# First attention stage: ScalarE's instructions put in another order within a group of steps

## The chip, the cores and the metric

One NeuronCore of a Trainium2 chip runs the whole program. The metric is the device time of one execution in microseconds (us); the figure for a kernel is the median over several executions.

## The reference, cut to what matters

The input is 16 sequences of 256 tokens with 128 features, in float32.

```python
x = L0_attn_hidden_states                    # (16, 256, 128)
x = _layernorm(x + _L0_attn_ref(x, ...))     # first attention
x = _layernorm(x + _L0_ffn_ref(x, ...))      # two layers of local attention and a gated MLP
```

The first attention works on a gated convolution of its input and takes a softmax over each chunk of 64 keys by itself:

```python
h = _dynamic_conv(x)                         # three taps, times a gate made from the mean over tokens
q, k, v = heads(h @ w_q.T), heads(h @ w_k.T), heads(h @ w_v.T)   # 16 query heads, 4 key/value heads, 64 wide
scores = jnp.einsum('bhqd,bhckd->bhcqk', q, kc) * scale
w = jax.nn.softmax(scores, axis=-1)          # over the 64 keys of one chunk
chunk_out = jnp.einsum('bhcqk,bhckd->bhcqd', w, vc)
out = (chunk_out * sum_w).sum(axis=2) / (sum_w.sum(axis=2) + 1e-09)
return out @ w_o.T
```

## The kernel before, in words

The program has two stages. `stage_a` (L342) is the first attention with its convolution, residual and norm; the two layers follow it. The change touches the first stage alone.

**Tiling.** A step of the first stage is one tile of 128 queries and one key/value head, with its four query heads: 2 tiles by 4 heads make 8 steps a sequence. Two steps form a group, and the four groups of a sequence are called quarters 0 to 3. `pairs` (L410) walks over the 8 groups of a turn, which is two sequences. The turns are "first", "middle" (a hardware loop over most of them), "last", and "drain", which finishes what is late and runs beside the first work of the layers.

**Order.** Every engine has its own program, with its instructions in an order written out by hand; semaphores tie them together. In one group the engines do this, for step s and its neighbour s + 1, and for the steps that are late (`PV_LAG` = 6 steps, which is three groups back):

- TensorE (L1448 to L1466): transposes of late weights (`weights_turned`, L1382), the first "fills", transposes of the next late weights, the last fill, the scores of s and s + 1 (L1397), and the weighted values of both late steps (`values`, L1415).
- VectorE (L1130 to L1159): maximum (L1091) and subtraction (L1100) of s, then of s + 1, then the sums (L1083) of both exponentials and their reciprocal (L1070). In odd quarters it adds the residual (L1118) and takes the norm's statistics (L1125, L1128).
- GpSimd (L673 to L687): in quarter 0 the gate's denominator and the convolution's sums, in odd quarters the norm's reciprocal root (`closing_statistics`, L660 to L671), then the shares of the chunks (L617 to L632) and the two multiplications that normalise the exponentials (L655).
- ScalarE (`a_body`, L867 to L909): copies of transposed weights out of PSUM (`weights_copied`, L843), exponentials (L849), copies of the fills (`filled`, L869), copies of the weighted values (`values_weighted`, L857), the end of the norm (`closed`, L865), the convolution's taps (`middle_tap`, L795, and `outer_taps`, L799 and L800) and the gated input (L807).

**Fills.** A fill is work that prepares a coming sequence, or closes one, between the steps: projections of queries (L1357), keys (L1359) and values (L1361), the transposed input (L1340), the gate's matmul (L1347), and "out", the output projection (L1426). The table `A_FILLS` (L129) says which quarter does which: a first list that stands ahead of the second transposes, and a last one behind them.

```python
0: ([("q", 4, 2, 0), ("q", 4, 3, 0)], [("gate", 1, 0, 1)]),
1: ([("xT", 1, 0, 2), ("out", 1, 0, 0)], [("v", 1, 0, 0)]),
2: ([("q", 4, 0, 1), ("q", 4, 1, 1)], [("k", 2, 0, 1)]),
3: ([("out", 1, 0, 0)], [("k", 2, 1, 1)]),
```

ScalarE copies q, k, v and xT; it passes over "gate" and "out" (L873), which VectorE reads.

**Banks.** All fills and the weighted values share PSUM banks 6 and 7 in turn (`stage_a_banks`, L114), so each matmul that writes one waits in `bank_free` (L423) until the piece before the last has been read out. In quarters 2 and 0 the third fill (k or gate) waits so for ScalarE's copy of the first (a q); in quarter 1 the third fill (v) waits for the copy of the first (xT). "out" waits also for the copy of the late weighted values (L1424). Each transpose of four waits until ScalarE has copied what stood in banks 4 or 5 (L1379), and the scores wait for subtractions two steps back (L1394), which read banks 0 to 3.

Of the kernel before, what the change touches and what calls it, by code (L numbers as in the profile page):

```python
# [43 lines left out]
PV_LAG, OUT_LAG, XO_LAG, A_DRAIN = 6, 10, 12, 12  # L44
# [16 lines left out]
def wait(engine, sem, value):  # L61

    if isinstance(value, int) and value <= 0:
        return
    engine.wait_ge(sem, value)
# [48 lines left out]
def stage_a_banks():  # L114
# [14 lines left out]
A_FILLS = {  # L129
# [5 lines that stand above are left out]
# [37 lines left out]
def build(nc, t):  # L172

    ctx = ExitStack()
    with ctx:
# [166 lines left out]
        def stage_a(engine, body, pre=None):  # L342

            if pre:
                pre()
            body(0, "first")
            body(1, "middle")  # L350
            with engine.Fori(2, TURNS - 1) as i:
                body(i, "middle")
            body(TURNS - 1, "last")
# [56 lines left out]
        def pairs(turn):  # L410

            for s in range(0, A_STEPS if turn != "drain" else A_DRAIN, A_GROUP):
                yield (s, *divmod(s // A_GROUP, A_KV))

        def exists(turn, s, lag=0):

            return not (turn == "first" and s < lag) and not (turn == "drain" and s >= lag)

        def prepares(turn, p, ahead=1):

            return turn not in ("drain", "drain2") and not (turn == "last" and p + ahead >= PAIR)
# [361 lines left out]
        def _(act):  # L783
            def x_transposed(i, local, turn, b):

                act.wait_ge(made["xT"], b + 1)
                wait(act, taps_set, b)
                wait(act, wk_ctx_set, b)
                nc.scalar.activation(xT[:, 1:SEQ + 1], banks[6 + A_BANKS.bank("xT", local, turn)][:, 0:SEQ], ACT.Copy,
                                     accum_out=ctx_sum[:, :]).then_inc(read["xT"], 1)  # L790

            def middle_tap(b):

                act.wait_ge(read["xT"], b + 1)
                nc.scalar.activation(conv[:, 0, :], xT[:, 1:SEQ + 1], ACT.Identity, bias=bconv[:, 0:1], scale=wconv[:, 1:2])  # L795

            def outer_taps(b):

                nc.scalar.activation(conv[:, 1, :], xT[:, 0:SEQ], ACT.Copy, scale=wconv[:, 0:1])  # L799
                nc.scalar.activation(conv[:, 2, :], xT[:, 2:SEQ + 2], ACT.Copy, scale=wconv[:, 2:3]).then_inc(taps_set, 1)  # L800

            def gated_input(b):

                act.wait_ge(conv_set, 2 * b + 2)
                act.wait_ge(gate_step, GATE_STEPS * (b + 1))
                wait(act, made["v"], b)
                nc.scalar.activation(hT[:, :], conv[:, 2, :], ACT.Copy, scale=gate_sum[:, 0:1]).then_inc(hT_set, 1)  # L807

            def gate_exponential(b):
                act.wait_ge(read["gate"], b + 1)  # L810
                nc.scalar.activation(gate[:, 1, :], gate[:, 0, :], ACT.Exp, scale=-1.0).then_inc(gate_exp, 1)

            def projected(kind, i, local, turn, m, pb):

                index = A_BANKS.stride[kind] * i + local
                act.wait_ge(made[kind], index + 1)
                bank = banks[6 + A_BANKS.bank(kind, local, turn)]
                if kind == "q":
                    nc.scalar.activation(qT[pb][:, 2 * m:2 * m + 2, :], bank[:, :], ACT.Copy, scale=A_HD ** -0.5).then_inc(read[kind], 1)
                elif kind == "k":  # L820
                    nc.scalar.activation(kT[pb][:, 2 * m:2 * m + 2, :], bank[:, :], ACT.Copy).then_inc(read[kind], 1)
                else:
                    nc.scalar.activation(v[pb][:, :, :], bank[:, :], ACT.Copy).then_inc(read[kind], 1)
# [14 lines left out]
            def weights_copied(n, r):  # L838

                for hp in range(2):  # L840
                    act.wait_ge(wT_made, 2 * n + hp + 1)
                    wait(act, pv_done, 2 * (n - A_GROUP) + hp + 1)
                    nc.scalar.activation(wT[2 * r + hp][:, :, :, :], banks[4 + hp][:, :], ACT.Copy).then_inc(wT_read, 1)  # L843

            def exponentials(n, s):

                act.wait_ge(sub_done, n + 1)
                e = E[s % E_RING]
                nc.scalar.activation(e[:, :, :, :], e[:, :, :, :], ACT.Exp).then_inc(exp_done, 1)  # L849

            def values_weighted(i, late):

                n = A_STEPS * i + late
                at, og = divmod(late, A_KV)
                act.wait_ge(pv_done, 2 * n + 2)
                wait(act, made["out"], A_SLOTS * i + at - 1)
                nc.scalar.activation(oT[at % 2][:, 2 * og:2 * og + 2, :],  # L857
                                     banks[6 + A_BANKS.bank("o", late, "middle")][:, 0:2 * P], ACT.Copy).then_inc(read["o"], 1)

            def closed(i, at):  # L860

                j, r = A_SLOTS * i + at, at % 2
                act.wait_ge(shift_set, 2 * j + 2)
                wait(act, xo_out[r], 16 * (2 * i + at // 2))
                nc.scalar.activation(xo[r][:, :], y[r][:, :], ACT.Identity, bias=rstd[r][:, 3:4], scale=rstd[r][:, 1:2]).then_inc(xo_set, 1)  # L865

            def a_body(i, turn, beside=None):  # L867

                def filled(p, part):  # L869

                    for kind, per, m, ahead in part:
                        b = PAIR * i + p + ahead
                        if kind in ("gate", "out") or not prepares(turn, p, ahead):  # L873
                            continue
                        if kind == "xT":
                            x_transposed(i, p + ahead, turn, b)
                        else:
                            projected(kind, i, per * (p + ahead) + m, turn, m, (p + ahead) % PAIR)

                for s, p, quarter in pairs(turn):  # L880
                    n, late = A_STEPS * i + s, s - PV_LAG
                    if exists(turn, s, PV_LAG):
                        weights_copied(n - PV_LAG, 0)
                    if exists(turn, s, 1):
                        exponentials(n - 1, s - 1)
                    filled(p, A_FILLS[quarter][0])
                    if beside:
                        beside(s)
                    if exists(turn, s, PV_LAG):
                        weights_copied(n - PV_LAG + 1, 1)  # L890
                    filled(p, A_FILLS[quarter][1])
                    if beside:
                        beside(s + 1)
                    if quarter == 0 and prepares(turn, p):
                        gate_exponential(PAIR * i + p + 1)
                    if quarter == 1 and prepares(turn, p):
                        gated_input(PAIR * i + p + 1)
                    if exists(turn, s, PV_LAG):
                        values_weighted(i, late)
                    if exists(turn, s):  # L900
                        exponentials(n, s)
                    if exists(turn, s, PV_LAG):
                        values_weighted(i, late + 1)
                    if quarter % 2 == 0 and exists(turn, s, XO_LAG):
                        closed(i, (s - XO_LAG) // A_KV)
                    if quarter == 2 and prepares(turn, p, 2):
                        middle_tap(PAIR * i + p + 2)
                    if quarter == 0 and prepares(turn, p):
                        outer_taps(PAIR * i + p + 1)  # L909

            stage_a(act, a_body, pre)

            def layers_program():
# [797 lines left out]
```

## Time and profile before

| what | value |
|---|---|
| median of 3 executions | 1357.25 us (1355.5 to 1358.14) |
| the profiled execution | 1355.71 us |
| its span, first to last instruction | 1353.2 us |
| TensorE matmuls busy | 1216.0 us, 90% of the span |
| VectorE busy | 1125.9 us, 83% |
| GpSimd busy | 1068.6 us, 79% |
| ScalarE busy | 953.8 us, 70% |
| mean granted TensorE clock | 0.984 |

The span is one profiled execution; the time of that execution lies 2.5 us above its span. Busy shares are means over stages with different limits: the first attention fills roughly the first 616 us, and the layers start between 612 us and 641 us. Matmuls are pipelined, so a start-to-start distance tells more of TensorE than its busy time does.

### The profile page before, as it was taken

What the parts mean: (1) busy time and instruction counts of PE and PEld (TensorE: products, weight loads), DVE (VectorE), ACT (ScalarE), POOL (GpSimd) and SP (SyncE); (2) the same over time, 40 slices, a digit from 0 to 9 for tenths busy, and PEclk for the clock granted to TensorE, in tenths of its full rate; (3) what the DMA queues carried; (4) which work ended last, traced back from release to release, by engine and by line L of the source; (5) the groups of instructions that cost most, each with busy time, mean ns of one, the idle gap of its engine ahead of it and who ended that gap; (6) DMA issues with size and microseconds to landing.
All of it is one profiled execution on the core that took longest, in us unless ns stands there. A gap on an engine that the chain in (4) does not pass through costs nothing.

```text
span 1353.2 us, 37200 instructions
## 1 busy us (share of the span) xinstructions
PE 1216.0 (90%) x12352; PEld 985.1 (73%) x12352; DVE 1125.9 (83%) x2210; ACT 953.8 (70%) x1772; POOL 1068.6 (79%) x1431
## 2 busy tenths in 40 slices
PE   3899999999999999986789999999999999999985
PEld 2577777777777778775567777777777777777764
DVE  2788898898889888894888888888888898989873
ACT  3466766766766676664668888888888787878762
POOL 0876676666666666668899999999999999999971
PEclk9799999999999999998999999999999999999998
DMA  5000000000000000000211111211212212121110
GB/s 179 4 11 13 10 9 12 12 12 12 12 12 10 12 12 8 9 12 8 50 41 44 49 42 42 52 40 43 51 46 51 51 42 52 42 51 44 47 39 24
DMA packets 87053, 44.28 MB, mean 33 GB/s; under 512 B 43908, under 2 KB 80048, under 8 KB 86960
## 3 DMA queue, kind: packets, MB, share of 16 engines
q1 hardware_dynamic: 86960, 43.08, 12.4%
q8 instruction: 54, 0.88, 0.3%
q14 instruction: 39, 0.32, 0.1%
HBM read 19.99 MB, written 6.29 MB: 19 GB/s over the span
## 4 chain that ended last, share of the span: by engine, by line
POOL 28%; PE 26%; issue 19%; DVE 17%; ACT 6%; SPq 2%; DVEq 1%; ACTq 1%; POOLq 1%; DMA 0%
POOL rnorm L716 9%; POOL kT L705 7%; DVE probs L1100 6%; PE bank L1397 4%; POOL probs L766 4%; DVE mx L1091 3%; POOL kT L719 3%; PE bank L1426 2%; PE bank L1533 2%; PE bank L1359 2%; PE bank L1494 2%; PE bank L1512 2%; PE bank L1568 2%; DVE sums L1083 2%; SPq L473 2%
## 5 line engine op out<-in xcount | busy, mean ns | idle before, releaser
L655 POOL TENSOR_TENSOR probs<-probs,coef 128x1024 f32<-128x1024 f32 x128 | 240.9, 1904 | 5.0
L716 POOL TENSOR_TENSOR rnorm<-norm,halves 128x8 f32<-128x8 f32 x128 | 213.7, 1669 | 10.7
L1091 DVE TENSOR_REDUCE mx<-bank 128x8 f32<-128x512 f32 x256 | 164.2, 683 | 34.8 <-PE bank L1397 34.4
L849 ACT ACTIVATE probs<-probs 128x1024 f32<-128x1024 f32 x128 | 135.5, 1058 | 54.2 <-DVE probs L1100 54.1
L1083 DVE TENSOR_REDUCE sums<-probs 128x16 f32<-128x1024 f32 x128 | 154.2, 1213 | 22.4 <-ACT probs L849 22.4
L705 POOL TENSOR_TENSOR kT<-qT 128x512 f32<-128x512 f32 x128 | 163.6, 1278 | 6.9 <-DVE qT L1177 6.9
L1100 DVE TENSOR_TENSOR probs<-bank,mx 128x512 f32<-128x512 f32 x256 | 161.2, 672 | 0.0
L719 POOL TENSOR_TENSOR kT<-kT,rnorm 128x512 f32<-128x512 f32 x128 | 133.4, 1042 | 10.0
L1382 PE MATMUL bank<-ident,probs 128*128 128x128 f32 x1024 | 137.0, 277 | 4.8 <-ACT wT L843 4.8
L843 ACT ACTIVATE wT<-bank 128x512 f32<-128x512 f32 x256 | 138.0, 596 | 1.2 <-PE bank L1382 1.2
L857 ACT ACTIVATE oT<-bank 128x256 f32<-128x256 f32 x128 | 47.9, 374 | 125.8 <-PE bank L1415 125.8
L1295 DVE TENSOR_REDUCE fmx<-bank 128x4 f32<-128x512 f32 x128 | 82.4, 685 | 59.4 <-PE bank L1568 59.4
L1397 PE MATMUL bank<-kT,qT 64*128 64x256 f32 x1024 | 131.3, 397 | 0.0
L1382 PEld LDWEIGHTS bank<-ident,probs 128*128 128x128 f32 x1024 | 114.2, 142 | 20.0 <-issue 13.6
L1415 PE MATMUL bank<-wT,v 128*64 128x128 f32 x2048 | 125.9, 276 | 0.0
L1415 PEld LDWEIGHTS bank<-wT,v 128*64 128x64 f32 x2048 | 110.5, 137 | 21.1 <-issue 21.1
L1397 PEld LDWEIGHTS bank<-kT,qT 64*128 64x128 f32 x1024 | 96.0, 191 | 25.8 <-issue 16.2
L1512 PE MATMUL bank<-hT,w 128*128 128x256 f32 (+1 forms) x384 | 96.8, 388 | 3.8 <-DVE uT L1203 2.3
L1582 PE MATMUL bank<-ident,probs 128*128 128x128 f32 x512 | 69.8, 280 | 26.6 <-POOL probs L766 26.5
L1494 PE MATMUL bank<-wqkv_high,fhT_high 128*128 128x512 f32 x192 | 92.5, 482 | 0.3
L1582 PEld LDWEIGHTS bank<-ident,probs 128*128 128x128 f32 x512 | 56.7, 142 | 47.3 <-POOL probs L766 37.9
L1176 DVE TENSOR_TENSOR qT<-bank,table 128x512 f32<-128x512 f32 x128 | 87.1, 680 | 2.9 <-ACT qT L918 1.9
(130 smaller groups left out, 3107.2 us busy)
## 6 DMA issues: line engine op xcount, KB each, us to landing
probs<-f_v SPq DMA_DIRECT2D x96, 128.0 KB, 2.3
res<-stage_x SPq DMA_DIRECT2D x48, 128.0 KB, 3.7
xn<-in_x SPq DMA_DIRECT2D x16, 128.0 KB, 2.2
xr<-in_x SPq DMA_DIRECT2D x16, 128.0 KB, 2.1
stage_x<-xo SPq DMA_DIRECT2D x32, 64.0 KB, 1.6
hn<-stage_x SPq DMA_DIRECT2D x32, 64.0 KB
mn<-mid SPq DMA_DIRECT2D x64, 32.0 KB
stage_x<-yo SPq DMA_DIRECT2D x16, 128.0 KB, 2.1
```

Of the source, the lines that this page charges most:

```text
L655: nc.gpsimd.tensor_tensor(out=e[:, :, :, :], in0=e[:, :, :, :], in1=coef[r % 2][:, 2, A_REP * at:A_REP * (at + 1), :].unsqueeze(3).broadca ...
L705: nc.gpsimd.tensor_tensor(out=qk[m][:, :, :], in0=on_self[m % 2][:, :, :], in1=on_partner[m % 2][:, :, :], op=ALU.add).then_inc(added, 1)
L716: nc.gpsimd.tensor_tensor(out=rnorm[:, at], in0=norm2[:, 1, at], in1=halves[:, 0:F_HEADS], op=ALU.pow).then_inc(rnorm_set, 1)
L719: nc.gpsimd.tensor_tensor(out=qk[m][:, :, :], in0=qk[m][:, :, :], in1=rnorm[:, at].unsqueeze(2).broadcast_to([P, F_HEADS, F_HD]), op=ALU.m ...
L843: nc.scalar.activation(wT[2 * r + hp][:, :, :, :], banks[4 + hp][:, :], ACT.Copy).then_inc(wT_read, 1)
L849: nc.scalar.activation(e[:, :, :, :], e[:, :, :, :], ACT.Exp).then_inc(exp_done, 1)
L1083: nc.vector.tensor_reduce(sums[r][:, A_REP * at:A_REP * (at + 1), :], E[(s + at) % E_RING][:, :, :, :], AX.X, ALU.add).then_inc(sum_done, 1)
L1091: nc.vector.tensor_reduce(mx[s % 2][:, 2 * k:2 * k + 2, :], banks[2 * (s % 2) + k][:, :].rearrange("p (h c k) -> p h c k", h=2, c=CHUNKS), ...
L1100: ins = nc.vector.tensor_tensor(E[s % E_RING][:, 2 * k:2 * k + 2, :, :], banks[2 * (s % 2) + k][:, :].rearrange("p (h c k) -> p h c k", h= ...
L1382: ins = nc.tensor.transpose(banks[4 + hp][:, P * (2 * kb + hh):P * (2 * kb + hh + 1)], e[:, 2 * hh + hp, 2 * kb:2 * kb + 2, :], ident[:, :])
L1397: ins = nc.tensor.matmul(banks[2 * (s % 2) + h % 2][:, SEQ * (h // 2):SEQ * (h // 2 + 1)], qT[p][lo:lo + A_HD, 2 * g + h // 2, P * tile:P ...
L1415: ins = nc.tensor.matmul(bank[A_HD * hh:A_HD * (hh + 1), P * hp:P * (hp + 1)], v[ap][:, kb, A_HD * og:A_HD * (og + 1)], wT[2 * r + hp][:, ...
```

## The change

ScalarE's program is the only one that changes, and only the order of its instructions within a group. No instruction, wait or buffer is added or removed.

```diff
                     if exists(turn, s, PV_LAG):
                         weights_copied(n - PV_LAG, 0)
+                    filled(p, A_FILLS[quarter][0][:1])
                     if exists(turn, s, 1):
                         exponentials(n - 1, s - 1)
-                    filled(p, A_FILLS[quarter][0])
+                    filled(p, A_FILLS[quarter][0][1:])
                     if beside:
                         beside(s)
                     if exists(turn, s, PV_LAG):
@@
                         gate_exponential(PAIR * i + p + 1)
                     if quarter == 1 and prepares(turn, p):
                         gated_input(PAIR * i + p + 1)
-                    if exists(turn, s, PV_LAG):
-                        values_weighted(i, late)
-                    if exists(turn, s):
-                        exponentials(n, s)
-                    if exists(turn, s, PV_LAG):
-                        values_weighted(i, late + 1)
                     if quarter % 2 == 0 and exists(turn, s, XO_LAG):
                         closed(i, (s - XO_LAG) // A_KV)
                     if quarter == 2 and prepares(turn, p, 2):
                         middle_tap(PAIR * i + p + 2)
                     if quarter == 0 and prepares(turn, p):
                         outer_taps(PAIR * i + p + 1)
+                    if exists(turn, s, PV_LAG):
+                        values_weighted(i, late)
+                        values_weighted(i, late + 1)
+                    if exists(turn, s):
+                        exponentials(n, s)
```

In words: the copy of a group's first fill stands ahead of the exponential of step s - 1 instead of behind it (in quarter 3 the first fill is "out", so nothing moves there). The norm's end and the taps stand ahead of the copies of the weighted values. The exponential of step s stands behind both of these copies instead of between them.

## Rows read from the trace of the kernel before

**Rows 1.** Windows view: busy PE, PEld, DVE, ACT, POOL; granted clock, DMA share, GB/s

```profile
260.00:330.00 70.00, 65.32 (x621) 55.14 (x621) 62.31 (x115) 47.21 (x90) 46.05 (x84) 1.00 0.04 10
```

**Rows 2.** View of waits, 120 to 612 us: total us, times, longest

```profile
ACT oT L857 <- PE bank L1415: 109.5, 54, 2.4
...
DVE mx L1091 <- PE bank L1397: 25.1, 37, 1.1
DVE sums L1083 <- ACT probs L849: 20.1, 27, 1.0
...
PE bank L1359 <- ACT qT L819: 10.3, 13, 0.8
PE bank L1347 <- ACT qT L819: 9.7, 12, 0.9
PE bank L1426 <- ACT oT L857: 8.4, 21, 1.8
...
PE bank L1361 <- ACT xT L789: 4.9, 11, 0.5
```

**Rows 3.** Timeline of TensorE, quarters 2 and 3 of one sequence: start, duration, work

```profile
303.05 1.04 PE L1382 MATMUL bank<-ident,probs 128*128 128x128 f32 x8
...
304.88 1.13 PE L1359 MATMUL bank<-hT,wk 128*128 128x256 f32 x4 [0.79 <-ACT qT L819]
...
305.94 2.00 PE L1397 MATMUL bank<-kT,qT 64*128 64x256 f32 x16
...
307.86 1.97 PE L1415 MATMUL bank<-wT,v 128*64 128x128 f32 x32
...
309.76 1.09 PE L1382 MATMUL bank<-ident,probs 128*128 128x128 f32 x8
...
311.09 2.05 PE L1426 MATMUL bank<-wo,oT 128*128 128x128 f32 x16 [0.23 <-ACT oT L857]
...
312.98 1.04 PE L1382 MATMUL bank<-ident,probs 128*128 128x128 f32 x8
...
313.85 1.03 PE L1359 MATMUL bank<-hT,wk 128*128 128x256 f32 x4
```

**Rows 4.** Timeline of ScalarE over the same quarters

```profile
303.28 1.06 ACT L849 ACTIVATE probs<-probs 128x1024 f32<-128x1024 f32 x1 [0.65 <-DVE probs L1100]
304.24 1.06 ACT L819 ACTIVATE qT<-bank 128x512 f32<-128x512 f32 x2
...
309.00 0.38 ACT L857 ACTIVATE oT<-bank 128x256 f32<-128x256 f32 x1 [2.23 <-PE bank L1415]
...
309.70 1.06 ACT L849 ACTIVATE probs<-probs 128x1024 f32<-128x1024 f32 x1 [0.32 <-DVE probs L1100]
...
310.67 0.36 ACT L857 ACTIVATE oT<-bank 128x256 f32<-128x256 f32 x1
...
310.93 0.48 ACT L865 ACTIVATE xo<-y,rstd 128x128 f32<-128x128 f32 x1
...
311.81 1.06 ACT L843 ACTIVATE wT<-bank 128x512 f32<-128x512 f32 x2
```

**Rows 5.** Timeline of VectorE and GpSimd over the same quarters

```profile
304.64 0.19 POOL L671 TENSOR_TENSOR rstd<-rstd 128x1 f32<-128x1 f32 x1
...
307.12 1.29 DVE L1091 TENSOR_REDUCE mx<-bank 128x8 f32<-128x512 f32 x2 [1.14 <-PE bank L1397]
...
308.43 1.24 DVE L1100 TENSOR_TENSOR probs<-bank,mx 128x512 f32<-128x512 f32 x2
```

**Rows 6.** Timeline of VectorE: the gate's reciprocal, once a sequence (the first and the last of 14)

```profile
76.75 0.12 DVE L1054 RECIPROCAL gate<-gate 128x3 f32<-128x3 f32 x1
...
553.52 0.12 DVE L1054 RECIPROCAL gate<-gate 128x3 f32<-128x3 f32 x1
```

**Rows 7.** Timelines at the two ends of the stage: VectorE and GpSimd

```profile
69.75 0.20 DVE L1075 RECIPROCAL total<-total 128x8 f32<-128x8 f32 x1 [1.03 <-POOL total L623]
...
616.02 3.76 POOL L655 TENSOR_TENSOR probs<-probs,coef 128x1024 f32<-128x1024 f32 x2
```

## The prediction

> **What bounds the kernel now.** I read the windows view first. In the steady part of the first attention TensorE has a matmul running for 65.3 of 70 us, VectorE is busy for 62.3, ScalarE for 47.2 and GpSimd for 46.1, at a granted clock of 1.00 [rows 1]. So two engines are nearly full and the other two have a third of the time free. The next view is that of waits between 120 and 612 us: TensorE sits idle for ScalarE alone, 10.3 us ahead of the key projection, 9.7 us ahead of the gate's matmul, 8.4 us ahead of "out" and 4.9 us ahead of the value projection, 33.3 us in all; VectorE sits idle for 25.1 us until scores are there and 20.1 us until an exponential is [rows 2]. ScalarE itself idles for 109.5 us ahead of the first copy of weighted values [rows 2]. It is late where TensorE needs it and has nothing to do a moment later: its order is what costs, not its work.
>
> The gate's reciprocal comes once a sequence, and from the first to the last of 14 rows there are 13 periods: (553.52 - 76.75) / 13 = 36.67 us a sequence [rows 6]. The stretch of 492 us behind the sums of rows 2 is 13.4 sequences.
>
> The timeline shows the pattern. In quarter 2 the keys' projection starts at 304.88, 0.79 us idle, behind ScalarE's copy of the first q, which starts at 304.24 because it is queued behind an exponential that itself waited 0.65 us for VectorE [rows 3, 4]. In quarter 3 "out" starts at 311.09 behind the copy of the second weighted values at 310.67, which is queued behind the exponential at 309.70 [rows 3, 4].
>
> **What a removed wait is worth.** The idle time shown understates it, since a wait also breaks the pipelining. I use start to start. Second transposes followed without a wait: 313.85 - 312.98 = 0.87 us; with it: 304.88 - 303.05 = 1.83. That is 0.96, and the projection then takes 1.06 until the scores (305.94 - 304.88), where an unhindered one takes about 0.96, so 1.06 us for this wait [rows 3]. "Out" in quarter 3 starts 1.33 us behind the transposes' start, where about 0.9 would do: 0.4 [rows 3]. The gate's wait (9.7 us over 12 times) is of the keys' kind, 1.0 us. In quarter 1 "out" and the value projection (4.9 us over 11 times) wait about 0.4 each by the view of waits [rows 2], and with the same 0.1 to 0.2 on top of each it is 1.1 together. A sequence loses 1.06 + 0.4 + 1.0 + 1.1 = 3.6 us on TensorE, and its floor is 36.67 - 3.6 = 33.1 us.
>
> VectorE's floor comes from its waits: (25.1 + 20.1) / 13.4 = 3.37 us a sequence, so 36.67 - 3.37 = 33.3 us [rows 2, 6]. The two floors are nearly one, and the higher one counts.
>
> **The change part by part.** I write S for the start of a group's scores; for the group at S = 305.94 the old order gives these offsets [rows 3, 4, 5]: maximum S + 1.18, subtraction of s done S + 3.73, weighted values S + 1.92 to S + 3.89, next group's transposes S + 3.82, first copy of weighted values S + 3.06, exponential S + 3.76, second copy S + 4.73, norm's end S + 4.99, copies of transposed weights S + 5.87 (with the norm's end and a tap in front; without them two less).
>
> *Exponential of s last.* The first copy starts 0.16 us behind the end of the first half of the weighted values (307.86 + 0.98, copy at 309.00) [rows 3, 4], so the second can start at S + 3.89 + 0.16 = S + 4.05. It is done by S + 4.4, and TensorE reaches "out" at S + 3.82 + 0.9 = S + 4.7 (with xT ahead of it later still). Both waits for "out" go. The exponential starts at S + 4.35 instead of S + 3.76, so 0.6 us later. VectorE wants it only behind the second subtraction, S + 6.0, and it ends at S + 5.4: no cost.
>
> *Norm's end and taps ahead.* They take 0.48 us and 0.4 to 0.5 a tap, and now fall into ScalarE's wait of 2.23 us at 309.00, which they leave shorter but not filled [rows 2, 4]. They could start at about 306.8; the row of GpSimd that they need ends at 304.83 [rows 5], a slack of 2.0 us. The transposed weights then start one exponential behind S + 4.35, at S + 5.3, instead of S + 5.87: 0.6 us earlier in quarters 3 and 1 (more in 1, which had two taps), 0.3 later in 0 and 2, where nothing stood in front. TensorE wants the first of the two banks at S + 6.5 at the earliest and the second 0.4 later; they are free at S + 5.9 and S + 6.4. The norm's store on SP's queue is issued earlier and delays nothing: DMA is busy 4% of this stretch [rows 1].
>
> *First fill ahead of the exponential of s - 1.* In quarters 2 and 0 that exponential waits for VectorE anyway (0.65 us at 303.28) [rows 4]. The q copy takes 0.59 us, starts at S + 6.3, and is out of the way at S + 6.8, when the subtraction it waited for lands (303.28 = S + 6.7 of its group). The exponential pays 0 to 0.1 us. The bank is free at S + 6.85; TensorE comes to its third fill at S + 7.4. Both waits, keys and gate, go. In quarter 1 the xT copy stands ahead in the same way and frees the value projection. VectorE's waits for exponentials sit mostly behind the taps and go too; the q copies that shift are covered by the 2.2 us that ScalarE idles later.
>
> So the TensorE waits go, and VectorE sets the pace. In quarter 0 it starts late. Its mean group is 33.3 / 4 = 8.3 us, and quarter 3 has more than the mean (residual, statistics, gate weights), I estimate 8.8; TensorE's mean is 8.3, and from quarter 3 to 0 it has the gate's small matmul in place of a projection (1.03 us [rows 3]), I estimate 7.6. So VectorE comes to the maximum up to 1.3 us behind S + 1.18, the exponential starts at up to S + 5.05 and the transposed weights are copied by S + 7.1, against S + 7.4, when TensorE wants their second bank in quarter 1. It holds, without much to spare. I add 0.1 us for it: 33.4 us a sequence, 3.27 saved.
>
> By the Trainium skill (Perfetto Trace Analysis, Identifying the Most-Contended Engine) matmul busy time is no measure of closeness to the limit and occupancy is a fair one for VectorE. By that rule VectorE alone is the engine to judge by; the start-to-start reading puts TensorE within 0.2 us of it. The sum would be 33.3 us by the rule and 33.4 by both.
>
> **Where it holds.** The start is set elsewhere: at 69.75 VectorE waits 1.03 us for GpSimd [rows 7], which splits weights beside its shares in the first turn. The last 40 us lack most fills and are VectorE's; one wait for "out" there gives about 1 us. The gain counts from 69.75 to about 575, (575 - 69.75) / 36.67 = 13.8 sequences. From the last multiplication at 616.02 [rows 7] GpSimd sets the pace and nothing moves against it. The sum: 13.8 x 3.27 + 1 = 46 us. The profiled execution took 1355.7 and would take 1309.7; the median lies 1.5 above it, so 1311. Bounds: if VectorE's small issue gaps close too, 33.0 a sequence, 51.6 saved, 1306, and 1301 with the first turn gaining 5; if a quarter of the gain is lost in coupling, 1323.
>
> **Rivals.**
> *The pace comes back through the late exponential* (a part of the gain is lost). VectorE lags in quarter 0, ScalarE now has the transposed weights and the first fill behind its exponential, and TensorE waits 0.4 us in each group at the transposes (L1382) or the third fill. Against: 0.3 us to spare by my offsets. For: two floors 0.2 us apart leave no slack to recover. 4 x 0.4 = 1.6 a sequence back: 13.8 x 1.7 = 23, so 1334.
> *Nothing is gained*: VectorE's idle 3.37 us are the tail of another loop and stay, and TensorE waits for VectorE in place of ScalarE. Against: every VectorE wait shown names TensorE's scores or a ScalarE exponential. 1357.
> *Slower*: the exponential last, 0.6 us later in all four groups, makes the copies of transposed weights late for the second transposes. It decides once the exponential starts past S + 5.1 in most groups; then TensorE waits at L1382 in each, and the fills behind it too. To end slower it must give back over 3.3 us, so more than 0.8 a group; with 1.1 a group, 13.8 x (4.4 - 3.27) = 16 slower, 1373. For it: the only thing that the change delays. Against: 0.5 us of slack in quarters 0 and 2.
>
> **Chances.** 0.65 the forecast, 0.23 the part gain, 0.05 nothing, 0.07 slower. About 0.2% is what a measurement of this kernel can tell from no change. Faster by more is 0.88, within it 0.05, slower 0.07. The range reaches from 1301 over the part gain to 1338. The likeliest case alone would be 1301 to 1323.
>
> **What the profile would show.** Right: a period near 33.4 us in the rows of the gate's reciprocal; TensorE's waits for the q, xT and oT copies under 5 us in all; the exponential of s starting 0.6 us later against its scores; VectorE busy about 97% of the steady stretch; the stage from 641 us on unchanged in length. Wrong: waits of TensorE at L1382 for ScalarE (the slower rival), VectorE still idle for exponentials, or a period above 35.

## The result, and the profile after

| | before | after |
|---|---|---|
| median of 4 executions each, us | 1356.66 (1355.5 to 1358.14) | 1305.13 (1303.14 to 1305.44) |
| ratio, 95% interval | | 0.9613 [0.9598, 0.9628] |
| the profiled execution, us | 1355.71 | 1305.02 |
| its span, us | 1353.2 | 1303.2 |

The kernel became 51.5 us faster. The forecast was 46 us, 1311 us, with a range of 1301 to 1338.

The windows view of the changed kernel, over the same stretch as [rows 1]: busy time of PE, PEld, DVE, ACT and POOL, then granted clock, share of DMA and GB/s.

```profile
260.00:330.00 70.00, 69.63 (x668) 60.53 (x665) 68.02 (x125) 54.49 (x102) 52.32 (x91) 1.00 0.04 11
```

TensorE went from 65.3 to 69.6 of 70 us, VectorE from 62.3 to 68.0. The view of waits of the changed kernel, 66 to 565 us, which is the first attention's main part there and answers to [rows 2] (total us, times, longest; a longer part of the stage than there, so a wait that is absent here is gone):

```profile
ACT oT L857 <- PE bank L1415: 79.2, 95, 2.4
...
ACT gate L811 <- DVE gate L1048: 10.3, 14, 1.1
PEld bank L1415 <- DVE y L1118: 8.6, 15, 1.0
...
PE bank L1415 <- DVE y L1118: 1.9, 6, 0.6
PE bank L1382 <- ACT wT L843: 1.8, 3, 1.0
...
DVE mx L1091 <- PE bank L1397: 0.2, 1, 0.2
```

The four waits of TensorE for ScalarE, 33.3 us in [rows 2], are gone, and so are both of VectorE's: the one for scores fell from 25.1 to 0.2 us, and the one for exponentials is on no row. Two small waits of TensorE are left. One is new: 1.9 us, and 8.6 us of its weight loads, for a bank that VectorE's residual addition (L1118) reads. The other, 1.8 us for transposed weights, stood at 2.7 us in the view of rows 2, in two waits of the drain.

The timeline of the changed kernel in quarters 2 and 3, which answers to [rows 3, 4]:

```profile
278.98 0.60 ACT L819 ACTIVATE qT<-bank 128x512 f32<-128x512 f32 x1
279.18 1.04 PE L1382 MATMUL bank<-ident,probs 128*128 128x128 f32 x8
...
280.01 1.06 ACT L849 ACTIVATE probs<-probs 128x1024 f32<-128x1024 f32 x1 [0.43 <-DVE probs L1100]
280.05 1.03 PE L1359 MATMUL bank<-hT,wk 128*128 128x256 f32 x4
...
281.01 2.00 PE L1397 MATMUL bank<-kT,qT 64*128 64x256 f32 x16
...
284.95 0.39 ACT L857 ACTIVATE oT<-bank 128x256 f32<-128x256 f32 x1 [0.49 <-PE bank L1415]
...
285.35 1.06 ACT L849 ACTIVATE probs<-probs 128x1024 f32<-128x1024 f32 x1
285.76 1.95 PE L1426 MATMUL bank<-wo,oT 128*128 128x128 f32 x16
```

The q copy is done while the exponential of s - 1 still waits for VectorE, and the key projection follows the transposes after 280.05 - 279.18 = 0.87 us, where it was 1.83. The second copy of weighted values ends at 285.34, before TensorE comes to "out" at 285.76. The exponential stands at S + 4.34 (S = 281.01).

The first and last mark of the gate's reciprocal in the changed kernel, as in [rows 6], and GpSimd's last multiplications of the stage with the first memset of the layers:

```profile
75.52 0.12 DVE L1054 RECIPROCAL gate<-gate 128x3 f32<-128x3 f32 x1
...
505.82 0.12 DVE L1054 RECIPROCAL gate<-gate 128x3 f32<-128x3 f32 x1
...
564.61 3.77 POOL L655 TENSOR_TENSOR probs<-probs,coef 128x1024 f32<-128x1024 f32 x2
...
589.31 0.52 POOL L735 MEMSET probs<- 64x512 f32 x1
```

The same memset in the kernel before:

```profile
639.85 0.52 POOL L735 MEMSET probs<- 64x512 f32 x1
```

Where the 50.0 us of the span came from, by these rows and [rows 6, 7]: 13 periods of 33.10 us in place of 36.67 give 46.5; up to the first mark 1.2; from the last mark to the last multiplications 62.5 - 58.8 = 3.7; from there to the end 737.2 became 738.6, which gives 1.4 back. Of these 1.4 us, 0.9 lie ahead of the memset (23.8 us became 24.7). In that stretch VectorE's first residual addition waits longer for "out"; the first row is of the kernel before, the second of the changed one:

```profile
617.38 0.29 DVE L1118 TENSOR_TENSOR y<-bank,xr 128x128 f32<-128x128 f32 x1 [1.80 <-PE bank L1426]
```

```profile
567.73 0.29 DVE L1118 TENSOR_TENSOR y<-bank,xr 128x128 f32<-128x128 f32 x1 [3.57 <-PE bank L1426]
```

Whether this wait is what makes the hand-over longer was not tried.

### The profile page after: what moved, and what is told of

Same layout as the page of the kernel before. It is cut to its first block, busy times and chain, and to the rows that moved or that the text cites. A ratio compares the mean times of both kernels' runs of the same rounds, so it can differ in the third digit from the quotient of the medians.

```text
span 1303.2 us, 37200 instructions
## 1 busy us (share of the span) xinstructions
PE 1200.7 (92%) x12352; PEld 984.2 (76%) x12352; DVE 1124.0 (86%) x2210; ACT 958.8 (74%) x1772; POOL 1070.0 (82%) x1431
## 4 chain that ended last, share of the span: by engine, by line
PE 39%; POOL 32%; DVE 14%; issue 11%; SPq 2%; ACT 1%; POOLq 1%; DVEq 0%; DMA 0%; ACTq 0%
POOL rnorm L716 11%; POOL kT L705 9%; PE bank L1415 7%; PE bank L1382 6%; PE bank L1397 6%; POOL probs L766 4%; DVE sums L1083 4%; POOL kT L719 3%; PE bank L1357 3%; DVE probs L1100 2%; PE bank L1426 2%; PE bank L1533 2%; PE bank L1359 2%; PE bank L1512 2%; PE bank L1568 2%
## 5 line engine op out<-in xcount | busy, mean ns | idle before, releaser
L1382 PE MATMUL bank<-ident,probs 128*128 128x128 f32 x1024 | 137.8, 278 | 10.1 <-ACT wT L843 7.4
L1382 PEld LDWEIGHTS bank<-ident,probs 128*128 128x128 f32 x1024 | 114.2, 142 | 26.0 <-issue 14.2
```

What stands on the lines that cost most here:

```text
L1382: ins = nc.tensor.transpose(banks[4 + hp][:, P * (2 * kb + hh):P * (2 * kb + hh + 1)], e[:, 2 * hh + hp, 2 * kb:2 * kb + 2, :], ident[:, :])
```

## The experiments

**Which part earns it.** Six kernels hold one or two of the three parts of the change. The edits against the kernel before are these, in ScalarE's `a_body`, shortened: calls stand without their conditions, and (closed, middle_tap, outer_taps) stands for the norm's end and the taps. "Fill" is the first hunk of the change, "taps" and "exponential" split the second.

```diff
# fill
+                    filled(p, A_FILLS[quarter][0][:1])
                     if exists(turn, s, 1):
                         exponentials(n - 1, s - 1)
-                    filled(p, A_FILLS[quarter][0])
+                    filled(p, A_FILLS[quarter][0][1:])
# taps: closed, middle_tap and outer_taps ahead, the rest in its old order
+                    (closed, middle_tap, outer_taps)
                     values_weighted(i, late)
                     exponentials(n, s)
                     values_weighted(i, late + 1)
-                    (closed, middle_tap, outer_taps)
# exponential: behind both copies, the taps still behind it
                     values_weighted(i, late)
-                    exponentials(n, s)
                     values_weighted(i, late + 1)
+                    exponentials(n, s)
                     (closed, middle_tap, outer_taps)
```

*Fill alone.*

> The first fill ahead of the exponential of s - 1, nothing else moved. My theory (each moved piece frees its own TensorE wait): the waits of the key projection and the gate's matmul for the q copy go, the value projection's wait for xT too, the waits of 'out' for the weighted values' copy stay. TensorE gains 1.06 + 1.0 + 0.5 = about 2.6 us of its 3.6 a sequence, but VectorE still waits about 1.5 us a sequence for exponentials queued behind the taps, so the period should be near 34.5 us and the time near 1326 us. Rival (the late second exponential is what paces everything): the period stays above 36 us and the time above 1345 us. Rival (the fill order alone is the change): the time is within 5 us of the full change's 1305.

*Taps alone.*

> The norm's end and the taps ahead of the copies of weighted values, the exponential of s still between the two copies, the fills in the old order. My theory: the transposed weights of quarters 3 and 1 are copied 0.4 to 1.3 us earlier, VectorE's waits for exponentials in those quarters shrink and the value projection's wait for xT goes, but the key, gate and 'out' waits stay: 0.6 us a sequence, about 8 us, near 1348 us. Rival (slack of ScalarE is what counts, wherever it comes from): a third or more of the full gain, 1340 us or less.

*Exponential alone.*

> The exponential of s behind both copies of weighted values, with the norm's end and taps still behind all of them, fills in the old order. My theory: the waits of 'out' go (0.9 us a sequence), the key and gate waits stay since their q copy still stands behind an exponential that waits for VectorE, and the transposed weights come 0.3 to 0.6 us later, so VectorE's exponentials in quarters 3 and 1 too: between 0 and 12 us gained, 1345 to 1357. Rival (slower through the late exponential): over 1360 us, with TensorE waits at L1382.

*Fill and taps, without the exponential.*

> The full change without its last part: the exponential of s stays between the two copies of weighted values. My theory: only the 'out' waits are left, 0.9 us a sequence, and VectorE's own limit of 33.1 hides none of it: period about 34.0, time about 1317 us. If the exponential's place is worth nothing, 1305 us; if it costs in the full change, below 1303.

*Fill and exponential, without the taps.*

> The full change without the move of the norm's end and the taps, which stay last, now behind the exponential of s. New theory after the first four runs: with the exponential of s between the two copies, every gain of TensorE makes VectorE late in quarter 0, the exponential waits for it, and 'out' waits for the exponential (its wait grew from 8.4 to over 19 us when the fills moved); the exponential last cuts that tie, so the parts don't add up. Then this kernel gains well more than the 18 + 8 us of its two parts alone. The taps behind the exponential make the transposed weights of quarters 3 and 1 0.9 to 1.7 us late and VectorE's exponentials with them, so it stays above the full change: about 1328 us. Rival (the parts simply add, and it is the taps with the exponential that give the surplus): 1332 us or more, with 'out' waiting no more and TensorE waiting at L1382 instead.

*Taps and exponential, without the fill.*

> The full change without the first fill ahead of the exponential of s - 1. Theory: the key and gate waits stay, about 1.0 us each a sequence, 'out' no longer waits; 2.1 x 13.8 = 29 us over the full change, about 1334 us, and VectorE keeps waiting for scores. Rival (the order of the fills matters only through the 'out' wait): within 10 us of 1305.

Measured, each against runs of the kernel before on the same chip (median 1357.66 us for the first four, 1357.21 for the last two); the period is the mean over 13 sequences by the gate's reciprocal:

| parts | median, us | ratio, 95% interval | period, us |
|---|---|---|---|
| fill | 1339.98 | 0.9868 [0.9848, 0.9888] | 35.6 |
| taps | 1347.74 | 0.9926 [0.9906, 0.9947] | 36.0 |
| exponential | 1349.45 | 0.9940 [0.9919, 0.9962] | 36.5 |
| fill, taps | 1332.81 | 0.9819 [0.9799, 0.9839] | 34.9 |
| fill, exponential | 1324.75 | 0.9766 [0.9750, 0.9782] | 34.5 |
| taps, exponential | 1334.14 | 0.9833 [0.9816, 0.9849] | 35.2 |
| all three | 1305.13 | 0.9613 [0.9598, 0.9628] | 33.1 |

Alone the parts gain 17.7, 9.9 and 8.2 us, 35.8 in all; together they gain 51.5. Fill with taps gains 24.9 us, less than the 27.6 of its two parts; the two pairs with the exponential gain more than their parts, 32.5 for 25.9 and 23.1 for 18.1. Taps alone, exponential alone and taps with exponential came out where the theory of the prediction, each removed wait priced by itself, had them. Fill alone (14 us over its expectation) and fill with taps (16 us over) did not. The view of waits of fill with taps, 120 to 560 us, says why (its lines carry numbers one higher):

```profile
PE bank L1427 <- ACT oT L857: 19.2, 25, 1.6
...
DVE mx L1092 <- PE bank L1398: 19.3, 24, 1.1
```

The key, gate and value waits are gone, but the wait of "out" grew from 8.4 us in the 492 us of rows 2 to 19.2 in 440. In fill alone, over the same 120 to 560 us, it had grown too:

```profile
PE bank L1427 <- ACT oT L857: 23.2, 25, 1.6
```

The timeline of fill with taps in a quarter 0 and the "out" that follows:

```profile
314.06 1.24 DVE L1101 TENSOR_TENSOR probs<-bank,mx 128x512 f32<-128x512 f32 x2
...
315.33 1.06 ACT L849 ACTIVATE probs<-probs 128x1024 f32<-128x1024 f32 x1 [0.75 <-DVE probs L1101]
316.29 0.36 ACT L857 ACTIVATE oT<-bank 128x256 f32<-128x256 f32 x1
...
316.82 2.05 PE L1427 MATMUL bank<-wo,oT 128*128 128x128 f32 x16 [1.55 <-ACT oT L857]
```

TensorE now reaches quarter 0 earlier than VectorE. The exponential of s waits 0.75 us for VectorE's subtraction, the second copy stands behind it, and "out" waits 1.55 us for that copy. So with the exponential between the two copies, time saved ahead of it is partly handed back at "out": VectorE's lateness reaches TensorE within the same group. With the exponential last it reaches TensorE only through the copies of the transposed weights, which TensorE wants 1.8 us later than "out" (303.76 and 301.93 in a quarter 0 of the changed kernel). The pair of kernels gives the price: they differ in the exponential's place alone, the wait of "out" goes from 19.2 us to none, and the time from 1332.8 to 1305.1, 28 us; on the old order the same move is worth 8.

Fill with exponential, expected at about 1328 us and measured at 1324.75, tests the same from the other side. Its view of waits, 120 to 550 us:

```profile
DVE sums L1083 <- ACT probs L849: 17.4, 25, 1.1
...
PE bank L1382 <- ACT wT L843: 11.0, 17, 1.1
```

"Out" waits no more, but the taps now stand between the exponential and the transposed weights, and TensorE waits for these (11.0 us) and VectorE for exponentials (17.4 us). This is the slower rival's mechanism, at the place that the prediction gave for it (L1382). The taps' move is what keeps it away from the full change, where the same wait is 1.0 us over 120 to 550 us. Taps with exponential kept the key and gate waits at 10.2 and 9.8 us (120 to 550 us), as expected, and came out at 1334.14 for an expected 1334.

**Which engine sets the pace now.** Two kernels add work to the changed one. On TensorE the first transpose of each bank is done twice (the inner loop's line becomes `if True:`):

```diff
-                    for kb in range(TILES):
-                        for hh in range(2):
+                    for kb, hh in [(0, 0)] + [(kb, hh) for kb in range(TILES) for hh in range(2)]:
```

> The changed kernel with the first transpose of each bank done twice: two more 128 x 128 transposes a step, 16 a sequence, at 0.11 us start to start, 1.75 us a sequence. If TensorE alone sets the pace now (it is busy for 69.6 of 70 us), the whole stage pays: 15.5 x 1.75 = 27 us, 1332 us. If VectorE sets it (68.0 of 70 us), a third or less of that.

On VectorE one reduction into a new tile that nothing reads stands behind `total_inverted` in each group:

```diff
+                    nc.vector.tensor_reduce(spare[:, s // A_GROUP % 4:s // A_GROUP % 4 + 1], ident[:, :], AX.X, ALU.add)
```

> The changed kernel with one more reduction of a 128 x 128 tile on VectorE a group, about 0.25 us, so 1.0 us a sequence. If TensorE alone sets the pace, VectorE's 0.9 us of idle a sequence take it up: under 5 us more. If VectorE sets it: 14 us more, 1319 us.

Measured: more on TensorE 1327.54 us, ratio to before 0.9791 [0.9774, 0.9807]; more on VectorE 1311.70 us, ratio 0.9672 [0.9656, 0.9688]. Of the first, the windows view, and of the second, the reduction itself (duration min, median, max in ns):

```profile
260.00:330.00 70.00, 70.00 (x683) 61.39 (x680) 65.46 (x119) 51.89 (x98) 49.40 (x89) 1.00 0.04 13
```

```profile
L1145 DVE TENSOR_REDUCE spare<-ident x70: 230/234/277, 23.5 to 586.5; 128x1 f32<-128x128 f32 x70
```

What the added work costs its own engine, from start to start: ten transposes take 290.03 - 288.94 = 1.09 us where eight take 0.87, and there are eight such blocks in a sequence, so 8 x 0.22 = 1.75 us; the reduction takes 287.36 - 287.21 = 0.15 us, less than its duration of 0.234, so 4 x 0.15 = 0.6 us.

```profile
288.94 1.25 PE L1382 MATMUL bank<-ident,probs 128*128 128x128 f32 x10
290.03 1.03 PE L1359 MATMUL bank<-hT,wk 128*128 128x256 f32 x4
```

```profile
287.21 0.23 DVE L1145 TENSOR_REDUCE spare<-ident 128x1 f32<-128x128 f32 x1
287.36 1.28 DVE L1101 TENSOR_TENSOR probs<-bank,mx 128x512 f32<-128x512 f32 x2
```

The period rose from 33.10 to 34.53 us for 1.75 us more on TensorE, which is 82% of it. For 0.6 us more on VectorE it rose to 33.51, which is 68%. So both engines are within some tenths of a us of setting the pace: neither of the plain alternatives holds, and TensorE stands a little nearer to its own. The two runs also bound what each engine needs for a sequence. With more on TensorE no matmul waits for another engine in the view of waits (120 to 550 us), while VectorE waits again for scores, 18.8 us in all:

```profile
DVE mx L1091 <- PE bank L1397: 18.8, 26, 1.0
```

TensorE alone would thus need 34.53 - 1.75 = 32.8 us. VectorE, by the other run, needs at most 33.51 - 0.6 = 32.9. The changed kernel takes 33.1, and its rows show where TensorE loses most of its 0.3 us: at the weighted values that follow the scores of quarter 1. They start 307.94 - 305.70 = 2.24 us behind the scores there, and 1.93 us behind them one group later.

```profile
305.70 2.00 PE L1397 MATMUL bank<-kT,qT 64*128 64x256 f32 x16
307.94 1.97 PE L1415 MATMUL bank<-wT,v 128*64 128x128 f32 x32 [0.24 <-DVE y L1118]
...
314.32 2.00 PE L1397 MATMUL bank<-kT,qT 64*128 64x256 f32 x16
316.25 1.97 PE L1415 MATMUL bank<-wT,v 128*64 128x128 f32 x32
```

They wait for the bank that VectorE's residual addition reads, and VectorE comes late to it. It is VectorE's lateness more than this one bank: the kernel with the early residual, below, has no such wait, and its period is still 33.01 us and not 32.8.

**Toward a faster version.** GpSimd's splitting of weights spread out, in the first turn:

```diff
-                        if turn == "first" and s + at < 3 * LAYERS:
-                            split_weights(*divmod(s + at, 3))
+                        if turn == "first" and at == 0 and s // A_GROUP < 3 * LAYERS:
+                            split_weights(*divmod(s // A_GROUP, 3))
```

> The changed kernel with GpSimd's splitting of the layers' weights spread over the first six groups of the first turn, one piece a group, instead of two pieces in each of the first three. In the changed kernel VectorE waits 1.99, 0.54 and 1.06 us for GpSimd there. If GpSimd's queue is what holds the start, 2 to 4 us come off, 1302 us; if the start is held by TensorE's half clock and the loads, nothing.

1303.53 us, ratio 0.9607 [0.9594, 0.9620]. The interval overlaps that of the changed kernel; a difference isn't shown.

The residual addition moved ahead of the sums of the group before:

```diff
-                    if closes:
-                        residual_added(i, (s - OUT_LAG) // A_KV)
...
+                    if quarter % 2 == 0 and exists(turn, s + A_GROUP, OUT_LAG):
+                        residual_added(i, (s + A_GROUP - OUT_LAG) // A_KV)
                     if exists(turn, s):
                         summed(n, s, j, r)
```

> The changed kernel with VectorE's residual addition moved from the start of the odd quarters to the end of the even ones, ahead of the sums, so that the bank that it reads is free sooner. In the changed kernel TensorE's weight loads for the weighted values wait for it 15 times, 8.6 us in all. Theory: TensorE sets the pace, so most of 0.2 us a wait comes off: 1 to 4 us. Rival: VectorE has no time left, the addition waits for 'out' and delays the sums: no gain or a loss.

1308.52 us, ratio 0.9645 [0.9632, 0.9658]: 3.4 us more than the changed kernel by the medians, with the intervals of the ratios apart, though TensorE's waits for L1118 were gone. Both edits together:

> Both edits. They touch different stretches, so their gains should add: 1299 to 1303 us.

1307.86 us, ratio 0.9636 [0.9623, 0.9649]: no better. The timelines of the early residual alone, at the end of the stage, show GpSimd's last multiplications and first memset, and VectorE's addition:

```profile
563.96 3.76 POOL L655 TENSOR_TENSOR probs<-probs,coef 128x1024 f32<-128x1024 f32 x2
591.54 0.52 POOL L735 MEMSET probs<- 64x512 f32 x1
```

```profile
579.87 0.29 DVE L1118 TENSOR_TENSOR y<-bank,xr 128x128 f32<-128x128 f32 x1 [6.96 <-PE bank L1426]
```

The stage's end came 0.65 us earlier than in the changed kernel (564.61), but the memset 2.2 us later (589.31). In the drain the addition waits 6.96 us for "out" with the layers' first work queued behind it. The last kernel has both edits and keeps the addition's old place there:

```diff
+                    if closes and turn == "drain":
+                        residual_added(i, (s - OUT_LAG) // A_KV)
...
-                    if quarter % 2 == 0 and exists(turn, s + A_GROUP, OUT_LAG):
+                    if turn != "drain" and quarter % 2 == 0 and exists(turn, s + A_GROUP, OUT_LAG):
```

> Both edits of the last run, but with the residual in its old place in the drain. In the two runs with the early residual the last multiplication of the stage came 0.65 and 2.3 us earlier than in the changed kernel, yet the layers' first memset 2.2 and 0.5 us later: in the drain the addition waits 3.7 and 7.0 us for 'out' with the layers' first work queued behind it on VectorE. Theory: with the old place there, the earlier end of the stage is kept: 2 to 3 us under the changed kernel, near 1302 us, ratio 0.958 to 0.960. Rival (the hand-over is late for another reason): near 1307.

```profile
561.93 3.77 POOL L655 TENSOR_TENSOR probs<-probs,coef 128x1024 f32<-128x1024 f32 x2
...
586.44 0.52 POOL L735 MEMSET probs<- 64x512 f32 x1
```

1302.71 us, ratio 0.9597 [0.9584, 0.9610], against 0.9636 [0.9623, 0.9649] for the same kernel with the drain's addition moved too. The two intervals lie apart, and from the last multiplications to the memset this kernel takes 586.44 - 561.93 = 24.5 us, as the changed kernel does (24.7), where each of the two kernels with the addition moved there took 27.6. This shows that the addition's place in the drain was the cause. The kernel has the fastest median of all, 2.4 us under the changed kernel, but the intervals of the two overlap, so that it beats the changed kernel is not shown. Nor is it shown that the early residual adds to the spread splitting: that kernel had 1303.53 us, and these intervals overlap too.

## Why the prediction was right

*What bounds the kernel, and the three moves.* Right. All four waits of TensorE for ScalarE went, as the row by row working had it, and both of VectorE's. VectorE was to be busy about 97% of the steady stretch, and was for 68.0 of 70 us. The exponential of s was put at S + 4.35 and came at S + 4.34. The q copy was to cost its exponential 0 to 0.1 us; at 280.01 that exponential still waits 0.43 us for VectorE, so it cost nothing there.

*Quarter 0, the tight spot.* The prediction put the exponential at up to S + 5.05 and the transposed weights within 0.3 us of being late. The rows of the changed kernel, scores of quarter 0 and what hangs on them:

```profile
296.95 2.00 PE L1397 MATMUL bank<-kT,qT 64*128 64x256 f32 x16
...
299.58 1.29 DVE L1091 TENSOR_REDUCE mx<-bank 128x8 f32<-128x512 f32 x2
...
302.17 1.06 ACT L849 ACTIVATE probs<-probs 128x1024 f32<-128x1024 f32 x1 [0.48 <-DVE probs L1100]
303.13 1.06 ACT L843 ACTIVATE wT<-bank 128x512 f32<-128x512 f32 x2
...
303.76 1.14 PE L1382 MATMUL bank<-ident,probs 128*128 128x128 f32 x8
```

VectorE's maximum stands 1.45 us behind its earliest place (S + 2.63 for S + 1.18), the exponential at S + 5.22. The copies end at 304.19, S + 7.24, and the transposes, which want the second bank half-way through, take 1.14 us in this sequence where others take 1.04: the slack is just used up. The estimate was 0.17 us short for the exponential and 0.14 for the copies, and cost at most the 0.1 us.

*The size.* Forecast 46 us, measured 50.7 between the profiled executions. The step that was mis-sized is "VectorE sets the pace", 33.3 us and 0.1 for coupling; the period is 33.10 us. VectorE's floor was its period less its named waits, which counts its small gaps as work. It was busy for 62.3 / 70 x 36.67 = 32.6 us a sequence before and 68.0 / 70 x 33.10 = 32.2 after, and the run with more on VectorE puts its need at 32.9 us at most, so the floor was at least 0.4 us too high. Over 13 periods the forecast saved 13 x 3.27 = 42.5 us and the kernel 46.5: 4 us.

TensorE's floor of 33.1 us agrees with the measured period by luck. The run with more on TensorE puts it at 32.8, so the loss from ScalarE's order was 3.9 us a sequence and not 3.6; and the 0.3 us above it show mostly as a wait for VectorE's residual addition, which the prediction does not name. Both floors were too high, and the coupling, put at 0.1, came to 0.2 or more over the higher of the two. Which of the two engines is the slower by itself the runs don't decide.

The other terms were small and partly cancel. Up to the first mark the forecast had 0.6 us and got 1.2; from the last mark on it had 1.9 us, the part of a sequence up to 575 us, and 1 us for the end, and got 3.7; the hand-over, put at nothing, took 1.4 back. The median was put 1.5 us above the profiled execution and came 0.1 above it, so that the forecast of 1311 lies 5.9 us above the measured 1305.1.

A slip in the working: the part gain was priced at 1.6 us a sequence, but multiplied as 1.7; by 1.6 it is 1333 instead of 1334, which changes nothing.

*The Trainium skill's rule.* The Trainium skill (Perfetto Trace Analysis, Identifying the Most-Contended Engine) calls matmul busy time a poor measure and names the weight loads' busy share, beside the arithmetic done, in its place. The prediction left that out. The loads were busy for 55.1 of 70 us before [rows 1] and 60.5 after, less than VectorE's 62.3 and 68.0, so by these shares VectorE comes first. The measurements agree in part. VectorE does follow closely, but the loads' 86% would leave TensorE 14% of the time, and the added work found it 0.3 of 33.1 us, 1%, from its limit. Here the start-to-start distances told TensorE's limit better.

*The rivals.* A part gain through the late exponential did not come (1334 us), though fill with exponential shows that its mechanism exists, once the taps stand behind the exponential. Nothing gained, and slower, did not come. What the prediction did not see is how the parts depend on each other. It priced each removed wait by itself, which would make fill and taps worth most of the change (1317 us expected, 1332.81 measured). The sum for all three came out right because with all three no wait was left to grow.

## What to carry to other kernels

A wait of a full engine for one that has idle time is a question of the second one's order: put what the full engine waits for ahead of what waits for something slower, and put instructions with slack into the idle stretch. Price the parts of a reordering together, not one by one, since an instruction that waits for a slow engine passes that wait to everything queued behind it, and the price grows as the other waits go. Take an engine's floor from start-to-start distances, and test it with added work where it counts: the period less its named waits was at least 0.4 us too high here, and estimated distances 0.3. State added work by what it costs from start to start as well; by its duration the reduction looked like 0.94 us a sequence and cost its engine 0.6.

## What the runs showed that I had not expected

Two engines within 3% of each other both charge for added work: 82% of it on one and 68% on the other, over 100% together. And an edit that shortened the steady part by 0.1 us a sequence, from 33.10 to 33.01 us, lost 3.4 us in all: one addition in the drain waited 6.96 us with the next stage's first work behind it.
